# Sorting swaps in pieces of 512 columns with one operand in PSUM, and fewer banks for an aggregation's sums

## The reference

```python
edge_index = jnp.stack([src, dst])
x = x + _L0_gnn_ref(_layernorm(x), src, dst, edge_weight, W, b)        # first aggregation
x = x + _L0_ffn_ref(_layernorm(x)[None], ...)[0]                        # eight experts, top 1
x = x + _L1_gnn_ref(_layernorm(x), edge_index, edge_weight, ...)        # second aggregation
x = x + _L1_ffn_ref(_layernorm(x)[None], ..., edge_index)[0]            # attention gates, four experts, top 2
```

## Time and profile before

| | |
|---|---|
| median of three runs | 9,416.56 us (9,409.66 to 9,444.65) |
| the profiled execution | 9,430.33 us |
| its span | 9,428.6 us |
| granted TensorE clock, mean | 0.753 |
| VectorE (DVE) busy | 4,478.7 us, 48% |
| POOL busy | 4,965.1 us, 53% |
| TensorE (PE) busy | 5,933.1 us, 63% |
| ScalarE (ACT) busy | 3,755.0 us, 40% |

### The profile page before, as it was taken

The page is one execution under the profiler, slowest core; times in us unless marked ns, Lnnn a source line. Parts: engine busy times, 40 slices in busy tenths (PEclk is TensorE's granted clock), DMA queues, the critical chain, the costliest instruction groups (busy, mean ns, idle before and its releaser), DMA issues. The chain is left out here.

```text
span 9428.6 us, 89657 instructions
## 1 busy us (share of the span) xinstructions
PE 5933.1 (63%) x20077; PEld 4003.3 (42%) x20077; DVE 4478.7 (48%) x8746; ACT 3755.0 (40%) x9688; POOL 4965.1 (53%) x4762
## 2 busy tenths in 40 slices
PE   5455555555569999655555555555647676777657
PEld 4333333333356666333433333333624444444446
DVE  6354455544569999564444444445712111212124
ACT  3455555555552222445554544555401111111114
POOL 3666666666442222546666666666454545454531
PEclk8666677767659999876776676667568788788778
DMA  5333333333321111543332222222321111111126
GB/s 140 99 97 99 101 101 101 95 90 90 94 102 41 50 54 41 139 148 88 90 89 83 86 83 84 85 83 85 131 55 43 40 42 41 42 40 46 40 74 252
DMA packets 500454, 797.43 MB, mean 85 GB/s; under 512 B 123070, under 2 KB 365355, under 8 KB 499851
## 3 DMA queue, kind: packets, MB, share of 16 engines
q0 software_dynamic: 200256, 453.47, 17.9%
q1 hardware_dynamic: 299696, 338.23, 11.0%
HBM read 595.60 MB, written 197.30 MB: 84 GB/s over the span
## 5 line engine op out<-in xcount | busy, mean ns | idle before, releaser
L935 PE MATMUL part<-rows,spread 128*128 x6656 | 2468.7, 527 | 2109.3 <-issue 1160.7
L935 PEld LDWEIGHTS part<-rows,spread 128*128 128x128 f32 x6656 | 1628.3, 262 | 2894.4 <-issue 2620.5
L892 DVE TENSOR_TENSOR agg<-agg,part 128x257 f32 (+1 forms) x3328 | 1404.6, 422 | 2398.6 <-issue 812.4
L875 POOL DMA_INDIRECT rows<-h,row x1563 | 1556.5, 996 | 878.5 <-issue 443.7
L875 POOL DMA_INDIRECT rows<-f,row x1563 | 1546.5, 989 | 801.3 <-issue 448.1
L959 ACT ACTIVATE spread<-iota,place 128x128 f32<-128x128 f32 x3328 | 1016.0, 387 | 2247.0 <-PE part L935 1108.2
L1878 POOL DMA_INDIRECT rows<-gat,src x1122 | 1059.6, 944 | 1097.6 <-DVEq L2065 764.8
L1953 PE MATMUL y_ps<-agg,hid 128*128 128x256 f32 x3136 | 889.0, 423 | 654.9 <-issue 650.3
L1953 PEld LDWEIGHTS y_ps<-agg,hid 128*128 128x128 f32 x3136 | 662.3, 212 | 902.3 <-issue 819.0
L965 ACT ACTIVATE spread<-spread,weight 128x128 f32<-128x128 f32 x3328 | 1017.4, 388 | 13.6
L2083 DVE TENSOR_TENSOR y_all<-y_ps,b 128x512 f32<-128x512 f32 x196 | 135.4, 691 | 1792.2 <-DMA h<-res 1044.2
(11 more groups left out here) (391 smaller groups left out, 6051.0 us busy)
## 6 DMA issues: line engine op xcount, KB each, us to landing
expert_rows<-y_all SPq DMA_DIRECT2D x196, 256.0 KB
made<-expert_rows SPq DMA_DIRECT2D x49, 1024.0 KB
x<-x SPq DMA_DIRECT2D x42, 896.0 KB
rows<-f,row POOLq DMA_INDIRECT x1563
rows<-h,row POOLq DMA_INDIRECT x1563
rows<-gat,src POOLq DMA_INDIRECT x1122
xbuf<-zero SPq DMA_DIRECT2D x128, 128.0 KB
x<-xbuf SPq DMA_DIRECT2D x32, 512.0 KB
```

Source lines behind the costliest of these rows:

```text
L875: pool.indirect_dma_start(out=rows[:, u, 0:D], out_offset=None, in_=table, in_offset=bass.IndirectOffsetOnAxis(ap=q.row[:, i:i + 1], axis= ...
L892: nc.vector.tensor_tensor(sum_t, sum_t, part[:, p % NB, 0:WIDE], ALU.add).then_inc(added, 1)
L935: nc.tensor.matmul(part[:, p % NB, 0:WIDE], spread[:, p % (2 * BANKS), :], row_p, start=True, stop=True).then_inc(multiplied, 1)
```

## The change

In a step before `lifted`, the halves of a swap are taken by pieces of 512 columns. For each piece the lower keys are copied to one of two PSUM banks (`lift`), and the mask, the minimum and the maximum read them there and the upper keys in SBUF. A half of 512 is one piece. `lifted` is the end of the list in the second aggregation's sorter and the last step within the first aggregation in the other. The two banks are taken from the sums: NB is 6 instead of 8, and 5 instead of 7. The selects stay as they are.

```diff
     def __init__(self, s, free, weighted, joined=False):
+        self.lift = None
...
+        self.lifted = len(self.steps) if joined else self.phase(free + 1)
         self.links, self.swaps, self.turns = [0], [0], [0]
         for i, (step, by) in enumerate(self.steps):
-            made = {"flip": 2 if 1 < by <= free else 1, "turn": self.pieces(i), "swap": 5 if weighted else 2}[step]
+            swap = (3 + weighted) * len(self.halves(i, by)) if i < self.lifted else 2 + weighted
+            made = {"flip": 2 if 1 < by <= free else 1, "turn": self.pieces(i), "swap": swap + 2 * weighted}[step]
...
+    def halves(self, i, by):
+        half = self.width(i) // 2
+        if half <= 512:
+            return [(0, slice(None), slice(None))]
+        if by <= 512:
+            return [(h, slice(h * 512 // by, (h + 1) * 512 // by), slice(None)) for h in range(half // 512)]
+        return [(h, slice(None), slice(h * 512, (h + 1) * 512)) for h in range(half // 512)]
...
             a, b = (v[:, :].rearrange("p (m h d) -> p m h d", h=2, d=by) for v in (key, w.key[1 - side][:, 0:n]))
-            if w.weighted:
-                m = w.mask[:, :].rearrange("p (m d) -> p m d", d=by)
-                link(nc.vector.tensor_tensor(m, a[:, :, 0, :], a[:, :, 1, :], ALU.is_gt))
-            link(nc.vector.tensor_tensor(b[:, :, 0, :], a[:, :, 0, :], a[:, :, 1, :], ALU.min))
-            link(nc.vector.tensor_tensor(b[:, :, 1, :], a[:, :, 0, :], a[:, :, 1, :], ALU.max))
+            m = w.mask[:, :].rearrange("p (m d) -> p m d", d=by) if w.weighted else None
+            for h, ms, ds in w.halves(i, by) if i < w.lifted else [(0, slice(None), slice(None))]:
+                low, high = a[:, ms, 0, ds], a[:, ms, 1, ds]
+                if i < w.lifted:
+                    own = low
+                    low = w.lift[:, h % 2, 0:min(n // 2, 512)].rearrange("p (m d) -> p m d", d=min(by, 512))
+                    link(nc.vector.tensor_copy(low, own))
+                if w.weighted:
+                    link(nc.vector.tensor_tensor(m[:, ms, ds], low, high, ALU.is_gt))
+                link(nc.vector.tensor_tensor(b[:, ms, 0, ds], low, high, ALU.min))
+                link(nc.vector.tensor_tensor(b[:, ms, 1, ds], low, high, ALU.max))
...
-        NB = BANKS if last_i is None else BANKS - 1
+        NB = BANKS - 2 if last_i is None else BANKS - 3
+        w.lift = s.ps("lift", [P, 2, 512])
```

## The result

The changed kernel took 9,705.0 us (median of 4 runs, 9,670.2 to 9,726.6) against 9,417.3 us for the kernel before (median of 4; one run more than in the table). The ratio is 1.029, with a 95% interval of 1.026 to 1.032: 288 us slower. The forecast was 9,440 us with a range that ended at 9,590.

A forecast was written before the change was run, and what follows sets the result against it. The ring of gathers, paced upstream of VectorE, was taken to bound the aggregations; 27 + 12 + 11 + 11 - 33 = +28 us on the profiled 9,430.3 gave 9,458, adjusted to the median 9,444, stated 9,440; range 9,350 to 9,590.

The forecast's parts named there:

- The durations: VectorE's sort: 512-element pieces and copies into PSUM take about 0.69 us each, adding 132 and 142 us in the two aggregations.
- The reading of the ring: Both aggregations: POOL waits for SP's free slots, SP for TensorE's products; the ring's pace is set upstream of VectorE.
- The first rival: Both aggregations: VectorE joins the path, TensorE standing longer at swaps, 218 and 85 us; at half price about 9,560; chance 0.26.
- How much lands on the path?: Key swaps in both aggregations: about a tenth of added swap time shows, +27 us; upper end +105 in the first alone.
- Priced at the same tenth: Fewer PSUM banks for the sums: 66 + 18 swaps at 1.3 us, a tenth of it showing, +11 us.
- the stretches of the kernel before: First aggregation in sixteen-gather stretches: 22.9 us without swap, 23.5 with fast selects, 25.4 with slow; 6.4 us more VectorE costs 0.6.
- The upper end of the banks: Fewer banks for the sums: at most 84 swaps at the full 1.3 us, 109 us.
- The relief: POOL's gathers beside key operations no longer stretched: 67 us, half taken, -33 us; ends 0 and -67.
- the third rival: Gathers in the aggregations: one that no longer meets a key operation meets the select behind it; +61 us, 9,478; chance 0.10.
- The row of SP at 1.39 us for one register instruction: First aggregation, shortly before POOL restarts: SP's register work stretches to 1.39 us, read as sequencers slow while gathers stream.

The follow-up runs named there:

- s0: Kernel before with register loads meant to make TensorE late; the loads were dropped in building, so it equals the kernel before: ratio 1.0001, undelayed sequencers.
- s3: Changed kernel with the same register loads, also dropped in building, so it equals the changed kernel: ratio 0.9951 to the kernel before, undelayed sequencers.
- fifth set: Two runs against the kernel before: pieces with copies within SBUF, six and five banks, 1.0228; changed kernel with one copy bank, seven and six, 1.0179.

## Why the prediction was wrong

**Right.** The durations: 0.69 us for every piece and for the copy, and VectorE busier by 257 us against 274. The copies number 321, not 318 (132 in the first aggregation, 189 in the second), which changes nothing. The reading of the ring: POOL waits for SP, SP for TensorE. One sign of being wrong was named and came: POOL's waits for SP grew by over 100 us, from 302 to 454.

**The first rival** had the direction and nearly the sum: 218 us for the first aggregation and 85 us for the second, together 303, where 182 and 111 came, together 293. Part of that is luck, since the two misses offset each other. For the second aggregation its mechanism is also not borne out: it had the 3.1 us hold fit into five banks (3.3 us) and only the longer 3.8 us outgrow them, but five banks with the old sort already cost 76 us there.

**The step that failed** is "How much lands on the path?", together with "Priced at the same tenth" for the banks. I took a tenth from the stretches of the kernel before and carried it over to microseconds that come on top of a hold which already outlasted the banks. The table in the section on the result gives the price on both sides. Eight banks take 5.2 us of products, six take 3.9. Before, the holds of 6.4 and 8.8 us outlasted the banks by 1.2 and 3.6 us and cost 0.3 and 0.9 us of a round. After, 8.4 and 10.8 us outlast them by 4.5 and 6.9 us and cost 2.6 and 3.8. So of the 3.3 us added to a swap round, 2.6 and 3.2 us showed, not 0.3. The price was no fixed share: the first 2 to 3 us beyond the banks cost little (my estimate from these four pairs), and what came after cost nearly in full. The other steps tell what each part cost: banks 145 us for the 11 in the sum; pieces with the short copy 45 us; the changed kernel's longer copy some 60 us net of the relief. The banks' 86 us in the first aggregation lie beside 66 x 1.3 = 86, but not by that alone: swap rounds there grew by 1.0 us (fast selects) and 1.5 us (slow), and rounds without a swap by 0.5.

**The upper end of the banks** was too low as well: 109 us for 66 + 18 holds, where 145 came, 76 of them in the second aggregation, which holds TensorE in every group by tally and sort together. I counted only its 18 merges. And I halved the rival's price without a row that said half. At its full price the range would have held the result.

**The relief**, taken at half of 67 us: POOL's busy time fell by 49. The 67 itself rested on a wrong reading. The gather of 1.59 us in the earlier trace rows that I put down to a key operation began beside the tally's comparison:

```profile
4367.15 0.95 DVE L767 TENSOR_TENSOR hot<-places,fields 128x1536 bf16<-128x1536 bf16 x1
```

Counted again by the operation that ran when a stretched gather began, the second aggregation has 51 us beside that comparison and 26 beside key operations, where I had 31 and 46; 20 + 26 = 46 us could go. Of those the 26 went, and 16 of the comparison's; in the first aggregation the mask's 20 went and 15 came back beside the selects. So the third rival, a gather that meets the select instead, was right in the first aggregation and wrong in the second, where no select follows. In time the relief brought no gain that shows with delayed sequencers, and up to 42 us in the second aggregation with undelayed ones. Here the Trainium skill's rule (SBUF — State Buffer, section Who interferes with whom) held in its first half: an instruction with two SBUF inputs contends with GpSimd's reads. Its inference that generating descriptors does not suffer is not what these runs show: beside key operations with two SBUF inputs the second aggregation's gathers were stretched by 35 us in all, and by none once one input was in PSUM (s0 and s3).

**Evidence I had and did not weigh.** The row of SP at 1.39 us for one register instruction stood in the prediction. I read it as a pace that nothing here changes. In every set with such rows fewer banks cost time, and in the two sets without them they cost none. That they are what leaves TensorE without slack is argued from this, not shown by a run of its own.

**Still open.** What delays the sequencers, and so which of the two verdicts a given execution will meet. How the second aggregation loses 76 us to the banks. Neither kernel is better under both: the change loses 2.9% with delayed sequencers and gains 0.5% with undelayed ones. With one bank for the copies it gains the same 0.5% there (0.9948) and loses 1.8%. Pieces in PSUM for the second aggregation alone, with one bank, were not tried; from the fifth set's traces I would expect them to lose little or nothing with delayed sequencers.

## What to carry to other kernels

A buffer between two engines hides a hold up to some length, and a slope measured below that length says nothing of the price above it. Compute hold minus the buffer's depth in time, before and after, for every kind of hold. Here 1.2 and 3.6 us beyond the depth cost 0.3 and 0.9 us, 4.5 and 6.9 us cost 2.6 and 3.8, so an addition on top of a hold that already outlasts the buffer is to be priced at its full length until a row says less. When rounds are averaged by what is in them, begin each at the same event, and try other beginnings before a small difference is used. And when sequencer instructions are stretched in a trace, test small buffers in both conditions: here they cost 1.5% in one and nothing in the other.

## What the runs showed of the hardware that I had not expected

The same kernel took 9,355 to 9,434 us in some sets of runs and 7,833 or 7,834 us in others. With undelayed sequencers all 3,136 of SP's landing instructions took 17 ns; with delayed ones they took up to 1,413 ns. The additions (422 ns) and the key operations have the same median durations in both.

A copy of 512 fp32 elements takes 437 ns within SBUF and 691 ns into PSUM. Moving one operand to PSUM hardly changes the length of the VectorE instruction that reads it (in the first aggregation 691 ns against 692 to 698), but it changes what the instruction does to POOL beside it.

What a VectorE instruction does to gathers depends on when they begin. Interleaving the kernel before's sort with its additions raised the first aggregation's gathers from 989 to 1,041 ns with the same operations.
